# A gated delta-rule attention on one core: gate exponentials, the system's matrix and the attention weights at other places in the round

## The chip, the cores and the metric

The kernel runs on one core of a Trainium2 chip. Its time is the device time of one execution in microseconds; the median of several executions is compared. In a profile PE is TensorE (matmuls; PEld its weight loads), DVE is VectorE, ACT is ScalarE, POOL is GpSimd, and SP is SyncE, which here only issues DMAs. Each engine works through its own instructions in the order in which the program has them, and waits at semaphores that the others raise.

## The reference

Inputs are `x` (4 x 512 x 512), a side tensor of the same shape, a conditioning vector for each batch, and the weights. Two blocks are added to `x`: a mixing recurrence followed by a gated delta-rule attention (16 query/key heads, 32 value heads, head size 128), and the mixing recurrence again followed by a binarised linear layer. The kernel spends most of its time in the attention:

```python
q, k, v = conv4_silu(x @ Wq), conv4_silu(x @ Wk), conv4_silu(x @ Wv)    # causal, 4 taps
beta, g = sigmoid(b), -exp(A_log) * softplus(a + dt_bias)
q, k = rmsnorm(q), rmsnorm(k)                                           # scaled
decay = where(lower triangle, exp(g_i - g_j), 0)                        # g summed in the chunk
M = where(strictly lower, (beta * k) @ k.T * decay, 0)                  # the system's matrix
T = inverse(eye + M)
# over the chunks, with a state of 128 x 128:
v_new = T @ (beta * v) - (T @ (beta * k * exp(g))) @ state
out   = (q * exp(g)) @ state + (q @ k.T * decay) @ v_new                # attention weights
state = state * exp(g_last) + (k * exp(g_last - g)).T @ v_new
y = x + (rmsnorm(out) * norm_w * silu(z)) @ W_out
```

The reference takes chunks of 64 positions. The kernel computes the same sums with chunks of 128.

## The kernel before

The attention is a loop over 64 items, an item being one of 16 head groups (one query/key head with two value heads) of one of 4 batches. Each item has three stages, and a round of the loop does one stage each of three items: stage L of item `l` (query and key: projection, convolution, gates, the system's matrix), stage A of item `m` = `l` - 1 (value and gate projections, the inverse of the system), stage B of item `n` = `l` - 2 (the recurrence over 4 chunks, norm, output projection). There are 66 rounds; in all but the first and the last two all stages are there. `b` is the round's number modulo 4. It selects extra work for the second mixing block: `mix_exps` in rounds with b = 0, `mix_scale` (two copies) with b = 1, `mix_forward` and `mix_sums` with b = 2, `mix_inverse` (a logarithm, a copy and an exponential, with two loads of tables) and `mix_ratio` with b = 3. POOL splits the weights of `z` for a new head group at the start of a round with b = 1.

The order is written by hand. Every engine has a `body(l, m, n, b)`, on ACT and DVE with slots `k` = 0 to 19. The order of the rest of a round on PE is: the hops of the recurrence (`hop_u`, `hop_os`, `hop_kq`) between quarters of the projections of v and qk, then those of z, then, from slot 9 on, the 11 products of the inversion with output projections (`out`) and other small pieces between them. Product `j` stands in slot `9 + j`, and each needs the one before it, after its result has been brought from PSUM to SBUF. Products 4, 6, 7, 9 and 10 (`ADDED`) are finished by DVE (`finish_product`, lines 1180 to 1193), the others are copied by ACT (line 999), each for the two heads apart. Product 5 makes the fourth power (`lower` times `s2`, copied into `slot` `s0`), and product 6 waits for its copy, though it does not read it; products 6 and 7 are the last two corrections of the inverse (`pinv`), product 8 turns it, product 9 is the residual, and product 10 ends the inverse, which `hop_u` of the next round reads.

What builds the system and the gates for item `l`, in the second half of its round:

- `exp_decay` and `exp_small` on ACT (lines 938 to 970) turn the masked gates `gb` into `decay` in place, after a table load, and make two small vectors.
- `b_matrix` on DVE (lines 1161 to 1173) makes `kks` from the key products and then, for each head, the four blocks of `bt`, and raises `b_ready`.
- `attention_weights` on DVE (line 1177) multiplies the query-key products in PSUM bank `rc` by `decay`, and raises `attn_ready`.
- `off_blocks` on POOL (line 1297) makes `lower` from `bt`. SP's `gather_blocks` (lines 612 and 615) sends the 16 x 16 diagonal blocks to HBM and back as `block_in`. POOL's `invert_blocks` (lines 1321 to 1328) inverts them, and in the next round SP's `scatter_blocks` (lines 620 and 627) sends the inverses to HBM and back into `inv16`. Product 0 of the next round waits for them.
- SP's `load_gates` for the next item waits for `attn_ready`. POOL's `mask_gates` and, at b = 1, `split("z", ...)` stand behind `invert_blocks`.

The waits on which the order rests:

```python
pe.wait_ge(S["inv16_loaded"], (m + 1) * (16 * NB))     # product 0
W({"v": "wv_split", "z": "wz_split"}[kind], it // BATCH + 1)   # first quarter of v or z
await_product(pe, m, h, k - 1)                         # products 1 to 10
```

Of the kernel before, what the change touches and what calls it, by code (L numbers as in the profile page):

```python
# [475 lines left out]
def attention_phase(nc, ctx, t):  # L476

    with ExitStack() as c:
# [182 lines left out]
        def _(pe):  # L661
# [154 lines left out]
            def body(l, m, n, b):  # L816


                L, A, B, p = l is not None, m is not None, n is not None, b % 2

                def hop(f, ch):
                    if B:
                        f(n, p, ch)

                def proj(kind, i, *ks):
                    if (L if kind == "qk" else A):
                        for k in ks:
                            proj_quarter(kind, i, k, m, n, l, p if kind == "qk" else 1 - p)
# [3 lines left out]
                        out_half(n, m, l, j, h)  # L832

                proj("v", 0, 0, 1)
                if A:
                    W("attn_ready", 2 * m + 2)
                hop(hop_u, 0)
                proj("v", 0, 2, 3)
                hop(hop_os, 0)
                proj("v", 1, 0)  # L840
                hop(hop_kq, 1)
# [57 lines left out]
        def _(act):  # L899
# [88 lines left out]
            def body(l, m, n, b):  # L988
# [4 lines left out]
                for k in range(SLOTS):  # L993
# [19 lines left out]
                    if L:  # L1013
                        if k == 4:
                            tap0("qk", l, 0)
                        elif k == 6:
                            tap0("qk", l, 1)
                        elif k == 7:
                            if B:
                                W("kq_full", 3 * n + 3)  # L1020
                            silu("qk", l, 0, qkT2[p][:, 1, :])
                        elif k == 8:
                            silu("qk", l, 1, qkT2[p][:, 0, :])
                        elif k == 10:
                            query_squares(l)
                        elif k == 12:
                            exp_decay(l)
                        elif k == 13:
                            exp_small(l, p)
                    if A:  # L1030
                        if k == 8:
# [22 lines left out]
        def _(dve):  # L1054
            v = nc.vector
# [162 lines left out]
            def body(l, m, n, b):  # L1218
                L, A, B, p = l is not None, m is not None, n is not None, b % 2
                if A:  # L1220
                    dve.drain()
                    v_columns(m)
                if L:
                    qk_columns(l)
                for k in range(SLOTS):
# [27 lines left out]
                    if L:  # L1253
                        if k == 5:
                            conv_tap("qk", l, 0, 1)
                            conv_tap("qk", l, 0, 2)
                        elif k == 6:
                            conv_tap("qk", l, 0, 3)
                        elif k == 7:
                            conv_tap("qk", l, 1, 1)  # L1260
                            conv_tap("qk", l, 1, 2)
                        elif k == 8:
                            conv_tap("qk", l, 1, 3)
                        elif k == 10:
                            if b == 1:
                                mix_backward(*mix_unit(l))
                            elif b == 2:
                                mix_forward(*mix_unit(l))
                            key_sums(l)
                        elif k == 12:  # L1270
                            query_sums(l)
                            small(l, p)
                        elif k == 13:
                            b_matrix(l, 0, p)
                        elif k == 14:
                            b_matrix(l, 1, p)
                        elif k == 16:
                            attention_weights(l, 0, p)
                        elif k == 17:
                            attention_weights(l, 1, p)  # L1280
                    if B and k in (15, 16, 17):
                        add_out(n, {15: 0, 16: 1, 17: 2}[k])

# [306 lines left out]
```

## Time and profile before

| | us |
|---|---|
| median of three runs | 3532.75 |
| lowest and highest of them | 3524.03, 3534.42 |
| the profiled execution | 3526.48 |
| its span in the profile | 3524.8 |
| one round in the middle (product 0 to product 0) | 49.61 |

The profile's page gives busy time for each engine; over the span PE is busy for 3235.5 us (92%), DVE for 2574.7 us, ACT for 1981.9 us and POOL for 1597.5 us. A timeline lists instructions in order of time, with runs of like instructions merged: start, length from the first start to the last end, engine, line, what is written and read, count, and in brackets the idle time of the engine before it with what ended it. Instructions of one engine overlap a little in these records, so a row can start before the row above it has ended. The view of stretches gives busy time of each engine between two points in time and the granted clock of TensorE as a share of its full speed.

### The profile page before, as it was taken

Reading aid. Unit: us, or ns where it says so; the run is one execution under the profiler, and the core shown is the slowest. Engines: PE = TensorE matmul, PEld = TensorE weight load, DVE = VectorE, ACT = ScalarE, POOL = GpSimd, SP = SyncE. Lnnn points to the kernel's source line nnn. Section 1 sums busy time; section 2 is a strip of 40 time slices with the busy share of each in tenths; the row PEclk is TensorE's granted clock in tenths of the full one; section 3 lists DMA queues with packets and bytes.
Section 4 is the critical chain, followed back from the end, with each engine's and each line's share of the span. In section 5 each row is a group of like instructions: output and inputs, shape, how many; then the busy total and the mean of one; then the engine's idle time right before and its main releaser. Section 6 shows DMA issues by size and latency. Waiting matters only on the chain. (4 is left out here: it accounts for less than half of the span.)

```text
span 3524.8 us, 57286 instructions
## 1 busy us (share of the span) xinstructions
PE 3235.5 (92%) x18210; PEld 2523.2 (72%) x18210; DVE 2574.7 (73%) x5351; ACT 1981.9 (56%) x4826; POOL 1597.5 (45%) x2825
## 2 busy tenths in 40 slices
PE   0249999999999999999999999999999999999977
PEld 0237777777777777777777777777777777777753
DVE  7747777777777777777777777777777777777753
ACT  6735666555655665555555665555555665556531
POOL 7644535444454535444454535444454435444310
PEclk9989999999999999999999999999999999999998
DMA  3312222222222222222222222222222222322102
GB/s 120 119 53 76 84 75 68 76 80 76 72 64 81 85 75 63 82 79 73 73 66 81 85 74 60 85 78 72 69 72 81 85 74 57 83 83 69 51 8 107
DMA packets 295389, 265.68 MB, mean 75 GB/s; under 512 B 221584, under 2 KB 250384, under 8 KB 285840
## 3 DMA queue, kind: packets, MB, share of 16 engines
q1 hardware_dynamic: 286160, 131.99, 15.2%
q10 hardware_dynamic: 8928, 130.03, 10.0%
q8 instruction: 146, 2.39, 0.3%
q14 instruction: 155, 1.27, 0.1%
HBM read 232.30 MB, written 29.62 MB: 74 GB/s over the span
## 5 line engine op out<-in xcount | busy, mean ns | idle before, releaser
L689 PE MATMUL x<-xs,w_high 128*128 128x512 f32 x3072 | 1054.7, 424 | 24.0 <-POOL w_low L1338 13.6
L922 ACT ACTIVATE uvec<-rb,cpos 128x128 f32<-128x128 f32 x512 | 160.4, 364 | 861.9 <-PE rb L709 861.9
L689 PE MATMUL x<-xs,w_low 128*128 128x512 f32 x1536 | 608.5, 396 | 0.0
L689 PEld LDWEIGHTS x<-xs,w_high 128*128 128x128 f32 x3072 | 525.7, 191 | 88.0 <-POOL w_low L1338 14.0
L999 ACT ACTIVATE slot<-lane 128x512 fp32r<-128x512 f32 x640 | 363.5, 650 | 228.5 <-PE lane L813 228.5
L1321 POOL TENSOR_TENSOR block_step<-block_in 64x14 f32<-64x14 f32 (+6 forms) x896 | 231.2, 258 | 329.8 <-DMA block_in<-blocks_dram 208.5
L1378 POOL TENSOR_TENSOR rstd<-rarg,powers 128x8 f32<-128x8 f32 x64 | 106.1, 1657 | 529.5 <-DVE rarg L1115 529.5
L689 PEld LDWEIGHTS x<-xs,w_low 128*128 128x128 f32 x1536 | 289.8, 189 | 66.7
L813 PEld LDWEIGHTS lane<-pinv,slot 128*128 128x128 f32 x1536 | 199.7, 192 | 190.8 <-ACT slot L999 98.7
L1297 POOL TENSOR_TENSOR lower<-bt,offdiag 128x512 fp32r<-128x512 f32 x128 | 171.5, 1339 | 321.5 <-DVE bt L1171 321.5
L1078 DVE SCALAR_TENSOR_TENSOR cacc<-x,cwv,cacc 128x511 f32<-128x511 f32 (+2 forms) x384 | 281.7, 747 | 38.4 <-ACT cacc L909 3.7
L1078 DVE SCALAR_TENSOR_TENSOR cacc<-x,cwqk,cacc 128x511 f32<-128x511 f32 (+2 forms) x384 | 281.2, 745 | 27.1 <-ACT cacc L909 5.9
L1323 POOL TENSOR_TENSOR block_in<-block_in,block_step 64x14 f32<-64x14 f32 (+6 forms) x896 | 238.8, 267 | 131.1 <-issue 5.9
L813 PE MATMUL lane<-pinv,slot 128*128 128x128 f32 x1536 | 245.7, 299 | 51.8 <-ACT slot L999 47.0
L778 PE MATMUL x<-vT,w_out 128*128 128x512 f32 x512 | 278.4, 627 | 0.9 <-DVE vT L1159 0.9
L1104 DVE SCALAR_TENSOR_TENSOR wvec<-ra,egn,vtok 128x128 f32<-128x128 f32 x384 | 117.0, 346 | 171.0 <-PE ra L698 171.0
L1390 POOL TENSOR_TENSOR irk<-skt,powers 128x4 f32<-128x4 f32 x64 | 64.6, 1009 | 355.8 <-PE x L689 339.4
L1171 DVE SCALAR_TENSOR_TENSOR bt<-cacc,cneg,gb 128x128 f32<-128x128 f32 x512 | 210.8, 473 | 5.6 <-ACT gb L945 0.9
L931 ACT ACTIVATE junk<-oraw 128x128 f32<-128x128 f32 x512 | 159.0, 311 | 39.4 <-issue 1.0
L1153 DVE TENSOR_TENSOR oraw<-oraw,rstd 128x1024 f32<-128x1024 f32 x64 | 129.0, 2016 | 61.3 <-POOL rstd L1378 61.3
L1311 POOL TENSOR_TENSOR gb<-gb,causal 128x512 f32<-128x512 f32 x128 | 164.7, 1287 | 18.5
L1185 DVE TENSOR_TENSOR pinv<-lane,inv 128x512 fp32r<-128x512 f32 x128 | 82.5, 686 | 117.3 <-PE lane L813 117.3
(230 smaller groups left out, 7474.6 us busy)
## 6 DMA issues: line engine op xcount, KB each, us to landing
xs<-mix_dram ACTq DMA_DIRECT2D x62, 2048.0 KB, 7.8
gb<-cum_dram SPq DMA_DIRECT2D x128, 256.0 KB, 4.4
w_in<-in_w_qkvz SPq DMA_DIRECT2D x48, 512.0 KB, 4.1
w_out<-in_w_out SPq DMA_DIRECT2D x16, 512.0 KB, 5.0
blocks_dram<-bt SPq DMA_DIRECT2D x512, 8.0 KB, 1.5
inverse_dram<-block_out SPq DMA_DIRECT2D x64, 128.0 KB, 2.2
inv<-inverse_dram SPq DMA_DIRECT2D x512, 16.0 KB, 1.8
xacc<-in_x SPq DMA_DIRECT2D x4, 1024.0 KB, 11.5
```

Source lines behind the costliest of these rows:

```text
L689: ins = mm(PROJ_BANK[kind][i][:, :], w, x, start=(k == 0 and j == 0), stop=(k == KC - 1 and j == 2))
L778: ins = mm(OUT_BANK[j][:, :], w_out[:, h, sl(j, P)], hT[:, h, :], start=(h == 0), stop=(h == HPG - 1))
L813: ins = mm(lane[h][:, sl(ch, CH)], a, b, start=True, stop=True)
L922: ins = a(uvec[:, h, :], rb[:, sl(h, HD)], ACT.Copy, scale=sm2[p]["cpos"][:, ch, h:h + 1])
L931: ins = a(junk[:, :], oraw[:, ch, h, :], ACT.Square, accum_out=sm["oss"][:, ch, h:h + 1])
L999: a(DEST[job][:, h, :, :].rearrange("p c s -> p (c s)"), lane[h][:, :], ACT.Copy).then_inc(copied[h], 1)
L1078: ins = v.scalar_tensor_tensor(out=cacc[:, i, j:SEQ], in0=PROJ_BANK[kind][i][:, 0:SEQ - j], scalar=weights[:, i, 3 - j:4 - j], in1=cacc[:, ...
L1171: ins = v.scalar_tensor_tensor(out=pair[p][:, h, ch, :], in0=kks[:, ch, :], scalar=sm["cneg"][:, ch, h:h + 1], in1=decay[:, h, ch, :], op0 ...
L1297: ins = g.tensor_tensor(lower[:, h, :, :], pair[p][:, h, :, :], t["offdiag"][:, :].unsqueeze(1).to_broadcast([P, NCH, CH]), ALU.mult)
L1311: g.tensor_tensor(x, x, t["causal"][:, :].unsqueeze(1).to_broadcast([P, NCH, CH]), ALU.add).then_inc(S["masked"], 1)
L1321: g.tensor_tensor(step, block_in[:, 0:i, i:i + 1].to_broadcast(shape), block_in[:, i:i + 1, i + 1:BLK].to_broadcast(shape), ALU.mult)
L1323: g.tensor_tensor(block_in[:, 0:i, i + 1:BLK], block_in[:, 0:i, i + 1:BLK], step, ALU.add)
```

## The change

Three pieces of work are written at another place, and one wait is moved.

- On ACT `exp_decay` and `exp_small` (slots 12 and 13) both stand in slot 14, behind the copy of product 5.
- On DVE `b_matrix` (slots 13 and 14) stands in slot 16 for both heads, behind the finish of product 7.
- On DVE `attention_weights` (slots 16 and 17) opens the next round, ahead of `v_columns`.
- PE's wait for `attn_ready` stands behind `hop_u` and the rest of the first v projection instead of ahead of it.

No instruction of an engine is added or removed, apart from the order.

```diff
@@ tensor, body
                 proj("v", 0, 0, 1)
+                hop(hop_u, 0)
+                proj("v", 0, 2, 3)
                 if A:
                     W("attn_ready", 2 * m + 2)
-                hop(hop_u, 0)
-                proj("v", 0, 2, 3)
                 hop(hop_os, 0)
@@ scalar, body
-                        elif k == 12:
+                        elif k == 14:
                             exp_decay(l)
-                        elif k == 13:
                             exp_small(l, p)
@@ vector, body
                 if A:
+                    attention_weights(m, 0, 1 - p)
+                    attention_weights(m, 1, 1 - p)
                     dve.drain()
                     v_columns(m)
@@ vector, body
-                        elif k == 13:
+                        elif k == 16:
                             b_matrix(l, 0, p)
-                        elif k == 14:
                             b_matrix(l, 1, p)
-                        elif k == 16:
-                            attention_weights(l, 0, p)
-                        elif k == 17:
-                            attention_weights(l, 1, p)
```

How it moves instructions on DVE, from the finish of product 4 (L1185) to the first vectors of the next round, in a round of the middle. Before (L1166 and L1171 are `b_matrix`, L1187 the finishes of products 6 and 7, L1216 `add_out`, L1177 the attention weights, L1189 and L1191 the finishes of products 9 and 10):

```order
L1185 TENSOR_TENSOR pinv<-lane,inv 128x512 x2
L1166 TENSOR_TENSOR cacc<-x,strict 128x512
L1171 SCALAR_TENSOR_TENSOR bt<-cacc,cneg,gb 128x128 x8
L1187 TENSOR_TENSOR pinv<-lane,pinv 128x512 x2
L1216 TENSOR_TENSOR xacc<-xacc,x 128x512
L1187 TENSOR_TENSOR pinv<-lane,pinv 128x512 x2
L1177 TENSOR_TENSOR attn<-rc,gb 128x512
L1216 TENSOR_TENSOR xacc<-xacc,x 128x512
L1177 TENSOR_TENSOR attn<-rc,gb 128x512
L1216 TENSOR_TENSOR xacc<-xacc,ra 128x512
L1189 TENSOR_TENSOR slot<-lane,slot 128x512 x2
```

The same place in the changed kernel, whose line numbers on DVE are lower by one:

```order
L1184 TENSOR_TENSOR pinv<-lane,inv 128x512 x2
L1186 TENSOR_TENSOR pinv<-lane,pinv 128x512 x2
L1215 TENSOR_TENSOR xacc<-xacc,x 128x512
L1186 TENSOR_TENSOR pinv<-lane,pinv 128x512 x2
L1165 TENSOR_TENSOR cacc<-x,strict 128x512
L1170 SCALAR_TENSOR_TENSOR bt<-cacc,cneg,gb 128x128 x8
L1215 TENSOR_TENSOR xacc<-xacc,x 128x512
L1215 TENSOR_TENSOR xacc<-xacc,ra 128x512
L1188 TENSOR_TENSOR slot<-lane,slot 128x512 x2
L1215 TENSOR_TENSOR xacc<-xacc,rb 128x512
L1190 SCALAR_TENSOR_TENSOR bt<-pinv,lane 128x512 x2
L1176 TENSOR_TENSOR attn<-rc,gb 128x512 x2
```

The nine instructions of `b_matrix` now stand between the finish of product 7 and that of product 9, and the two of the attention weights behind the finish of product 10.

On ACT, in a round with b = 3, from the copy of product 3 (L999 `lower`) to `mix_inverse` (L959 to L962). Before:

```order
L999 ACTIVATE lower<-lane 128x512 x2
L945 ACT_TABLE_LOAD
L945 ACTIVATE gb<-gb,gneg 128x128 x8
L969 ACTIVATE edec<-edd 128x8
L970 ACTIVATE egl<-glast 128x8
L999 ACTIVATE slot<-lane 128x512 x2
L959 ACT_TABLE_LOAD
```

The same place in the changed kernel:

```order
L999 ACTIVATE lower<-lane 128x512 x2
L999 ACTIVATE slot<-lane 128x512 x2
L945 ACT_TABLE_LOAD
L945 ACTIVATE gb<-gb,gneg 128x128 x8
L969 ACTIVATE edec<-edd 128x8
L970 ACTIVATE egl<-glast 128x8
L959 ACT_TABLE_LOAD
```

The copy of product 5 passes the table load and ten exponentials, which then stand directly ahead of the mixing block's work and the copy of product 8.

## Rows read from the trace of the kernel before

**Rows 1.** Waits: who waited, for whom, total us, times, longest.
```profile
PE lane L813 <- ACT slot L999: 47.0, 63, 2.2
```
**Rows 2.** Stretches, a round each: length, busy us (instructions) by engine, clock, DMA.
```profile
1499.16:1548.77 49.61, 48.79 (x283) 38.30 (x282) 37.70 (x82) 27.06 (x71) 20.55 (x43) 1.00 0.23 62
```
**Rows 3.** Timeline, PE, products 5 to 7, 9 and 10: start, length us.
```profile
1510.71 1.07 PE L778 MATMUL x<-vT,w_out 128*128 128x512 f32 x2
1511.21 1.41 PE L813 MATMUL lane<-slot,lower 128*128 128x128 f32 x8
1512.46 1.07 PE L778 MATMUL x<-vT,w_out 128*128 128x512 f32 x2
1514.25 1.14 PE L813 MATMUL lane<-pinv,slot 128*128 128x128 f32 x8 [0.72 <-ACT slot L999]
1515.23 1.07 PE L778 MATMUL x<-vT,w_out 128*128 128x512 f32 x2
1516.37 1.26 PE L813 MATMUL lane<-pinv,slot 128*128 128x128 f32 x8
...
1520.98 1.95 PE L813 MATMUL lane<-slot,bt 128*128 128x128 f32 x16
...
1523.23 1.40 PE L813 MATMUL lane<-pinv,slot 128*128 128x128 f32 x8
```
**Rows 4.** Timeline, ACT, the same round: table load, then the copy of product 5.
```profile
1509.78 1.28 ACT L945 ACT_TABLE_LOAD   x1
...
1513.63 1.06 ACT L999 ACTIVATE slot<-lane 128x512 fp32r<-128x512 f32 x2
```
**Rows 5.** Timeline, DVE, the same round.
```profile
1511.66 0.68 DVE L1166 TENSOR_TENSOR cacc<-x,strict 128x512 f32<-128x512 f32 x1
...
1515.64 1.27 DVE L1187 TENSOR_TENSOR pinv<-lane,pinv 128x512 fp32r<-128x512 f32 x2
1516.84 0.67 DVE L1216 TENSOR_TENSOR xacc<-xacc,x 128x512 f32<-128x512 f32 x1
1517.43 1.27 DVE L1187 TENSOR_TENSOR pinv<-lane,pinv 128x512 fp32r<-128x512 f32 x2
...
1522.08 0.69 DVE L1189 TENSOR_TENSOR slot<-lane,slot 128x512 fp32r<-128x512 f32 x1 [0.98 <-PE lane L813]
```
**Rows 6.** One line, the blocks of `bt`: duration of one, ns, min/median/max.
```profile
L1171 DVE SCALAR_TENSOR_TENSOR bt<-cacc,cneg,gb x512: 336/347/1372, 222.1 to 3352.4; 128x128 f32<-128x128 f32 x171
```
**Rows 7.** Timeline, ACT, next round (b = 3): `mix_inverse`, the copy of product 8.
```profile
1564.31 1.28 ACT L959 ACT_TABLE_LOAD   x1
...
1569.44 1.09 ACT L999 ACTIVATE slot<-lane 128x512 fp32r<-128x512 f32 x2 [0.61 <-PE lane L813]
```
**Rows 8.** Timeline, SP: gather and scatter in the b = 2 round.
```profile
1515.74 3.62 SPq L612 DMA_DIRECT2D blocks_dram<-bt  x8
...
1537.64 3.76 SPq L627 DMA_DIRECT2D inv<-inverse_dram  x8
```
**Rows 9.** Timeline, SP: the scatter that follows a b = 1 round.
```profile
1687.35 4.84 SPq L627 DMA_DIRECT2D inv<-inverse_dram  x8
```
**Rows 10.** DMA issues: count, KB, median us to landing.
```profile
inv<-inverse_dram SPq DMA_DIRECT2D x512, 16.0 KB, 1.8
```
**Rows 11.** Timelines, POOL and PE, start of a b = 1 round: z's split, z's projection.
```profile
1636.33 2.38 POOL L1338 TENSOR_TENSOR w_low<-w_in,w_high 128x1024 fp32r<-128x1024 f32 x1
```
```profile
1643.94 0.71 PE L689 MATMUL x<-xs,w_high 128*128 128x512 f32 x2
```
**Rows 12.** Stretches at half and full clock, columns as in rows 2.
```profile
202.94:206.36 3.42, 3.42 (x9) 2.64 (x9) 0.20 (x3) 0.00 (x0) 0.00 (x0) 0.50 0.44 113
267.80:271.20 3.40, 2.41 (x16) 2.05 (x16) 2.00 (x4) 3.37 (x8) 0.25 (x1) 1.00 0.99 323
271.20:281.40 10.20, 8.31 (x36) 7.98 (x37) 7.52 (x15) 4.60 (x12) 2.84 (x3) 0.50 0.34 120
3442.00:3445.60 3.60, 0.88 (x3) 0.05 (x1) 0.69 (x1) 0.00 (x0) 0.00 (x0) 1.00 0.18 15
```

## The prediction

> **What bounds the kernel now.** I read the waits first, then one round cut out of the middle, then the timeline of that round engine by engine. The waits name one place where TensorE's matmuls stop in 63 rounds for 47.0 us together: product 6 stands behind ACT's copy of product 5 [rows 1]. A round takes 49.61 us, TensorE is busy for 48.79 us of it and its granted clock is 1.00 [rows 2]. So TensorE sets the round, and a chain that stays in its shade costs nothing. Read the timeline of PE as pairs: an output projection (L778, two matmuls) and the product behind it. Unhindered, the product ends 1.91 us after its pair began (1510.71 to 1511.21 + 1.41 = 1512.62). Product 6 ends 2.93 us after its pair (1512.46 to 1515.39), product 7 2.40 us (1515.23 to 1517.63) [rows 3]. So 1.02 + 0.49 = 1.5 us of each round are lost there, more than the 0.72 us that the brackets show. The first loss is ACT's: it loads a table at 1509.78, works through the exponentials and turns to the copy at 1513.63, 3.85 us later [rows 4], though product 5 had ended at 1512.62. The second is DVE's: it starts the finish of product 6 at 1515.64, when `b_matrix` has ended [rows 5].
>
> All points in time below are those of this round, which begins with product 0 at 1499.16 and is a b = 2 round.
>
> **The copy of product 5 goes first (gain).** The first head of product 5 ends half a product before its end, so ACT copies from about 1512.2 to 1513.3 (1.06 us [rows 4]). Product 6 then finds its first head copied by 1512.8 and starts unhindered: it ends at 1512.46 + 1.91 = 1514.37. DVE, with `b_matrix` gone from its front, starts the finish of product 6 at about 1513.95, and product 7 ends at about 1516.13. The 1.5 us are won by then. What is late next decides how much is kept.
>
> **`b_matrix` behind the finish of product 7 (gives most of it back).** DVE from there: finish 6 at 1513.95, `add_out` 1.20 later at 1515.15, finish 7 0.59 later at 1515.74, `b_matrix` 1.20 later at 1516.94 [rows 5]. The exponentials end at 1513.3 + 3.85 = 1517.15, which the first block of `bt`, 0.75 us after the start, does not feel. `b_matrix` occupies DVE from 1511.66 to 1515.64, 3.98 us; so it is over at 1520.92 and `b_ready` comes at about 1521.0, against 1515.74, where the gather starts [rows 5, 8]: **5.26 us later**. Two `add_out` of 0.6 us follow, so the finish of product 9 starts at 1522.12 and ends 0.69 us later at 1522.81. TensorE, 1.5 us early, would have wanted to start product 10 at about 1521.75; it starts at 1522.87, waits again a little for the second head (finished 0.6 us after the first, at 1523.42), and ends 0.65 us after that, at 1524.1 instead of 1523.23 + 1.40 = 1524.63. A usual round therefore keeps **0.53 us** of the 1.5. The finish of product 10 then ends about 1525.2, just before `hop_u` would start.
>
> **Attention weights in the next round (nothing).** They cost DVE 2 x 0.6 us behind the finish of product 10 and end at about 1526.4. Only `hop_os` reads them, which on TensorE follows `hop_u`, its copy and half a projection, a microsecond later. DVE has 2.6 us idle there before its first hop. SP's load of the next gates waits for them, but the gates are not touched before POOL's inversion is over. I take zero, with an upper bound of 0.1 us a round.
>
> **ACT at b = 3 (loss).** There `mix_inverse` stands behind the exponentials. It starts at 1564.31 and ends 0.61 us before the copy of product 8 at 1569.44, so it takes 4.52 us [rows 7]; moved to the clock of the first round by 49.61 us, that copy starts at 1519.83. In the changed kernel ACT ends the exponentials at 1517.15 and `mix_inverse` at 1521.7, and the copy is 1.86 us later than before, where TensorE would have been 1.5 us earlier. Its first head ends at 1522.3, and product 9 starts at 1522.35 instead of 1520.98 [rows 3]. The rest runs as before: the round is **1.36 us longer**, with TensorE idle for some 2.6 us in it (from the output projection behind product 8, which ends at about 1519.7). At b = 0 and b = 1 the mixing work is short (`mix_exps`, two copies) and ends near 1518.5, in time.
>
> **The inverses' round trip.** It is rigid: gather, inversion, scatter, product 0. The last DMA of the scatter is issued about 0.45 us before 1537.64 + 3.76 = 1541.40 and lands 1.8 us later [rows 8, 10], at 1542.8, and product 0 of the next round starts at 1548.77 [rows 2]: 6.0 us of room. The move takes 5.26 and an earlier TensorE 0.53, so 0.2 us is left. From uneven landings I expect 0.08 us lost in a usual round, leaving 0.45. Behind b = 1 rounds the eight loads took 4.84 us instead of 3.76 [rows 9] and the gather was slower too: there the room is only 4.1 us. If that stays, that round has 5.26 + 0.53 - 4.1 = 1.7 us to wait. Both long groups fall on moments at which code is fetched, and those go with TensorE, not with `b_ready`, so I expect the slowness not to stay in this round.
>
> **z's weights at b = 1.** POOL's split stands behind the inversion and ended at 1638.71; z's first matmul started at 1643.94 [rows 11], 5.23 us later. Room 5.23 against 5.26 + 0.53: a stall of about 0.6 us, up to 1.2 if DMAs are slow there. This round interval changes by +0.1 to +0.6; I take +0.35.
>
> **The sum.** Of four rounds: two usual ones, -0.45 each; b = 3, +1.36; the one with z's split, +0.35. Over the attention: 16 x (-0.90 + 1.36) + 15 x 0.35 = **+12.6 us**.
>
> **TensorE's clock.** The idle 2.6 us at b = 3 are of a kind the trace shows at one place. In 267.80 to 271.20, with products alone and gaps, TensorE was busy for 2.41 us of 3.40, and the clock then fell to 0.50 of full, 1.2 GHz, for 10.2 us. After 0.88 us busy of 3.60 it fell too. The shortest stretch at the low level lasted 3.4 us [rows 12]. The full rounds, with a gap of 0.72 us, kept 1.00 [rows 2]. The new gap lies with the first group. A fall costs half of what it lasts, 1.7 to 5.1 us. TensorE has gapless work behind the gap, so I take 2.5 us, and that it happens in half of the 16 rounds: 8 x 2.5 = **+20 us**.
>
> The Trainium skill ("TensorE: Matmul & The Clock Gate", section "Why this matters for your kernels") warns of idle gaps between bursts of matmuls that are somewhat longer than the one I foresee. By that rule the clock would stay and the sum be +12.6; no row here has a gap of just this length.
>
> Together +32.6 us on the profiled execution's 3526.48 (its span is 3524.8; 1.7 us lie around it), that is 3559. That execution was at the low end of the runs; on the median of 3532.75 it gives **3565 us**.
>
> **Rivals.**
>
> 1. *The clock stays up.* All else as above: 3532.75 + 12.6 = 3545. For it: no fall anywhere between the second and the last round, and the skill's rule. Against it: rows 12. Chance 0.25.
>
> 2. *The round trip binds.* If the slow DMAs stay behind b = 1 rounds, each costs 1.7 us more, 16 x 1.7 = 27 us; if `b_ready` comes 0.5 us later than worked out, all four kinds of round feel it, 0.5 x 63 = 31 us. With half the clock's loss: 3573 to 3592. For it: only 0.2 us of room. Chance 0.15.
>
> 3. *Faster: `b_matrix` is short in its new place.* One block of `bt` takes 347 ns at the median and one of eight takes up to 1372 [rows 6], just while POOL begins `lower`. Were that pause absent, `b_matrix` would take 2.9 us. Then the finish of product 9 would be in time and usual rounds keep 1.5 us; with b = 3 unchanged the sum is 16 x (-1.5 x 2 - 1.1 + 1.36) = -44 us: 3489 before any fall of the clock, some 3505 with it. It decides from about 0.5 us less than 3.98. Against it: POOL starts `lower` on the first head's `b_ready` wherever that is, so the pause should move along. Chance 0.12.
>
> 4. *No change.* Stalls and gains cancel: the b = 3 copy is late by less than a microsecond. Chance 0.08, near 3533.
>
> **How the numbers follow.** My forecast has 0.40. The forecast and rival 2 are slower, 0.55, and so are four fifths of rival 1 (its 12.6 us have 6 to 20 around them, from z's stall and the loss in usual rounds), 0.20: 0.75 for slower by over 0.3%, which is 10.6 us and about what a measurement of this kernel can tell from no change. Same: 0.13. Faster: 0.12. The range leaves out rival 3 and the far end of rival 2: 3533 to 3590.
>
> **What would show it.** In the profile after: no wait of product 6 for ACT; product 10 waiting for the finish of product 9 for about 1.1 us in usual rounds; a row of 2.6 us idle before product 9 once in four rounds, ended by ACT's copy; z's first matmul waiting for POOL's `w_low` at b = 1; rounds of 49.1, 49.1, 51.0 and 49.9 us; granted clock below 1.00 in some of the b = 3 rounds. I would be wrong if the copy of product 8 is in time at b = 3, or if product 0 waits for DMAs in most rounds.

## The result and the profile after

| | before | after |
|---|---|---|
| median of four runs, us | 3532.24 | 3557.51 |
| lowest and highest, us | 3524.03, 3534.42 | 3553.84, 3561.81 |
| profiled execution, us | 3526.48 | 3553.84 |
| its span, us | 3524.8 | 3551.8 |

The change makes the kernel slower by 25 us; the ratio of the times is 1.0076 [1.0058, 1.0094]. The forecast was 3565 us with a range of 3533 to 3590.

The page of the changed kernel. TensorE is busy for 9.5 us less than before, and the span is 27.0 us longer:

```profile
PE 3226.0 (91%) x18210; PEld 2542.7 (72%) x18210; DVE 2567.7 (72%) x5351; ACT 1988.1 (56%) x4826; POOL 1585.7 (45%) x2825
```

Two rounds of it as stretches, product 0 to product 0, first one with b = 2, then one with b = 3 (columns as in rows 2):

```profile
2106.40:2155.05 48.65, 48.14 (x280) 38.30 (x281) 37.24 (x81) 26.51 (x70) 19.32 (x43) 1.00 0.24 73
2155.05:2207.59 52.54, 49.83 (x283) 39.48 (x282) 36.94 (x80) 31.49 (x76) 26.16 (x45) 0.97 0.29 78
```

This usual round is 1.0 us shorter than the 49.61 us of rows 2, the one with b = 3 is 2.9 us longer, and its granted clock is 0.97. The next table has all 62 rounds between the first product 0 that has a full round behind it and the last, taken from the starts of product 0 in the two traces. Falls are the stretches in which the granted clock is 0.50; "held" counts the rounds whose next product 0 starts less than 0.16 us after the last load of the inverses has landed:

| b | rounds | before, mean us | after, mean us | after, median us | falls after | held, before | held, after |
|---|---|---|---|---|---|---|---|
| 1 | 15 | 49.62 | 49.38 | 49.44 | 0 | 0 | 12 |
| 2 | 16 | 49.70 | 48.97 | 48.90 | 1 | 0 | 8 |
| 3 | 16 | 49.62 | 51.93 | 52.32 | 11 | 0 | 0 |
| 0 | 15 | 49.62 | 50.04 | 49.95 | 0 | 0 | 1 |

Together 15 x (-0.24) + 16 x (-0.73) + 16 x 2.31 + 15 x 0.42 = +28.0 us, against +27.0 in the spans.

The waits of the changed kernel (who waited, for whom, total us, times, longest). The 63 waits of rows 1 for the copy of product 5 are gone; what stands in their place is 17 waits for ACT, 46 for DVE's finish of product 9, 16 for POOL's split and 15 for the DMAs of the inverses:

```profile
PE lane L813 <- ACT slot L999: 43.5, 17, 2.7
...
PE x L689 <- POOL w_low L1334: 26.3, 16, 13.6
PE lane L813 <- DVE slot L1188: 22.6, 46, 0.8
...
PE lane L813 <- DMA inv<-inverse_dram: 8.7, 15, 1.4
```

The timeline of PE in the round from 2106.40, from product 6 to product 10 (it answers to rows 3). Products 6 and 7 each follow their pair by 0.51 us and end 1.92 us after it began; product 10 waits 0.48 us for DVE:

```profile
2119.45 1.07 PE L778 MATMUL x<-vT,w_out 128*128 128x512 f32 x2
2119.96 1.41 PE L813 MATMUL lane<-pinv,slot 128*128 128x128 f32 x8
2121.20 1.07 PE L778 MATMUL x<-vT,w_out 128*128 128x512 f32 x2
2121.71 1.41 PE L813 MATMUL lane<-pinv,slot 128*128 128x128 f32 x8
...
2126.47 1.95 PE L813 MATMUL lane<-slot,bt 128*128 128x128 f32 x16
2128.26 1.02 PE L778 MATMUL rb<-vT,w_out 128*128 128x512 f32 x2
2129.77 1.26 PE L813 MATMUL lane<-pinv,slot 128*128 128x128 f32 x8 [0.48 <-DVE slot L1188]
```

The timeline of DVE there (it answers to rows 5): finish 7, `kks`, the eight blocks of `bt`, two `add_out`, finish 9 without a pause between them:

```profile
2122.76 1.28 DVE L1186 TENSOR_TENSOR pinv<-lane,pinv 128x512 fp32r<-128x512 f32 x2
2123.96 0.68 DVE L1165 TENSOR_TENSOR cacc<-x,strict 128x512 f32<-128x512 f32 x1
2124.71 3.21 DVE L1170 SCALAR_TENSOR_TENSOR bt<-cacc,cneg,gb 128x128 f32<-128x128 f32 x8
2127.84 0.67 DVE L1215 TENSOR_TENSOR xacc<-xacc,x 128x512 f32<-128x512 f32 x1
2128.44 0.67 DVE L1215 TENSOR_TENSOR xacc<-xacc,ra 128x512 f32<-128x512 f32 x1
2129.04 1.27 DVE L1188 TENSOR_TENSOR slot<-lane,slot 128x512 fp32r<-128x512 f32 x2
```

The next round has b = 3. ACT's timeline, where three table loads stand in a row of work without a gap, ahead of the copy of product 8 (it answers to rows 4 and 7):

```profile
2168.08 1.08 ACT L999 ACTIVATE slot<-lane 128x512 fp32r<-128x512 f32 x2 [2.45 <-PE lane L813]
2169.18 1.28 ACT L945 ACT_TABLE_LOAD   x1
2170.48 2.45 ACT L945 ACTIVATE gb<-gb,gneg 128x128 f32<-128x128 f32 x8
...
2173.14 1.28 ACT L959 ACT_TABLE_LOAD   x1
...
2175.73 1.28 ACT L962 ACT_TABLE_LOAD   x1
...
2177.56 1.06 ACT L999 ACTIVATE slot<-lane 128x512 fp32r<-128x512 f32 x2
```

What TensorE does meanwhile, and the stretches at that place (columns as in rows 2). It idles for 2.68 us ahead of product 9, then 3.4 us go by at half the clock:

```profile
2174.44 1.07 PE L778 MATMUL rb<-vT,w_out 128*128 128x512 f32 x2
2178.19 3.01 PE L813 MATMUL lane<-slot,bt 128*128 128x128 f32 x16 [2.68 <-ACT slot L999]
```
```profile
2175.70:2179.10 3.40, 0.91 (x8) 0.91 (x9) 2.28 (x5) 2.88 (x4) 2.65 (x3) 1.00 0.08 8
2179.10:2182.50 3.40, 3.40 (x14) 2.57 (x12) 1.38 (x2) 0.00 (x0) 0.26 (x1) 0.50 0.11 11
```

### The profile page after: what moved, and what is told of

Same layout as the page of the kernel before. It is cut to its first block and busy times, and to the rows that moved or that the text cites. A ratio compares the mean times of both kernels' runs of the same rounds, so it can differ in the third digit from the quotient of the medians.

```text
span 3551.8 us, 57224 instructions
## 1 busy us (share of the span) xinstructions
PE 3226.0 (91%) x18210; PEld 2542.7 (72%) x18210; DVE 2567.7 (72%) x5351; ACT 1988.1 (56%) x4826; POOL 1585.7 (45%) x2825
## 5 line engine op out<-in xcount | busy, mean ns | idle before, releaser
L689 PE MATMUL x<-xs,w_high 128*128 128x512 f32 x3072 | 1054.8, 424 | 37.1 <-POOL w_low L1334 26.3
L999 ACT ACTIVATE slot<-lane 128x512 fp32r<-128x512 f32 x640 | 359.5, 636 | 194.0 <-PE lane L813 191.7
L813 PE MATMUL lane<-pinv,slot 128*128 128x128 f32 x1536 | 265.9, 313 | 22.8 <-DVE slot L1188 22.6
L1186 DVE TENSOR_TENSOR pinv<-lane,pinv 128x512 fp32r<-128x512 f32 x256 | 164.5, 683 | 141.9 <-PE lane L813 141.9
L813 PEld LDWEIGHTS lane<-slot,bt 128*128 128x128 f32 x1024 | 136.8, 210 | 79.4 <-ACT slot L999 68.2
L813 PE MATMUL lane<-slot,bt 128*128 128x128 f32 x1024 | 141.3, 297 | 43.5 <-ACT slot L999 43.5
```

The source lines that it names most:

```text
L689: ins = mm(PROJ_BANK[kind][i][:, :], w, x, start=(k == 0 and j == 0), stop=(k == KC - 1 and j == 2))
L813: ins = mm(lane[h][:, sl(ch, CH)], a, b, start=True, stop=True)
L999: a(DEST[job][:, h, :, :].rearrange("p c s -> p (c s)"), lane[h][:, :], ACT.Copy).then_inc(copied[h], 1)
L1186: ins = v.tensor_tensor(pinv[:, h, :, :], made, pinv[:, h, :, :], ALU.add)
```

## The experiments

Theory: four things make the time, which the runs below switch one by one. TensorE wins back the wait for the copy of product 5; ACT's mixing work at b = 3 opens a gap, and the gap makes the clock fall; POOL's split of z is late at b = 1; the round trip of the inverses has no room left. The rivals are that the gap alone costs and the clock nothing, and that `b_matrix` behind product 7 is the cause by itself. Ratios are to the kernel before on the same chip. A change against the changed kernel is the difference of the two ratios.

**The exponentials alone, in the kernel before.** `b_matrix` stays in slots 13 and 14.

```diff
-                        elif k == 12:
+                        elif k == 14:
                             exp_decay(l)
-                        elif k == 13:
                             exp_small(l, p)
```

> The kernel before with only ACT's part of the change: the exponentials in slot 14, behind the copy of product 5; the system's matrix stays in slots 13 and 14 on DVE, the attention weights in 16 and 17. Theory (the copy's place can be had only with the matrix moved): product 6 starts unhindered, but DVE stands in b_matrix until the exponentials are there, about 3.3 us later than before, and the finish of product 6 with it; TensorE idles some 3 us before product 7 in each round and its clock falls in most of them. 3.2 us a round and up to 1.6 for the clock: +200 to +300 us on the kernel before. Rival (the exponentials are what made the kernel slow, the matrix is free): like the changed kernel, +27 us.

3876.19 us, ratio 1.0981 [1.0947, 1.1014], +343 us. DVE's timeline: the first block of `bt` waits for the exponentials, with the finishes of product 6 queued behind it. PE's timeline: product 7 waits for them.

```profile
2029.62 0.68 DVE L1165 TENSOR_TENSOR cacc<-x,strict 128x512 f32<-128x512 f32 x1
2033.87 3.31 DVE L1170 SCALAR_TENSOR_TENSOR bt<-cacc,cneg,gb 128x128 f32<-128x128 f32 x8 [3.57 <-ACT gb L945]
2037.11 1.27 DVE L1186 TENSOR_TENSOR pinv<-lane,pinv 128x512 fp32r<-128x512 f32 x2
```
```profile
2037.84 1.81 PE L813 MATMUL lane<-pinv,slot 128*128 128x128 f32 x8 [4.60 <-DVE pinv L1186]
```

A round takes 55.0 us, 5.4 more than before, and each of the 62 has a fall of the clock. That is more than expected: TensorE idles 4.6 us before product 7 (290.7 us in 63 waits) where some 3 were foreseen, and 39 of 63 falls last 6.8 us where the working had 1.6 us of loss, one of 3.4. The first two pieces of the change are one: the exponentials can't go behind the copy unless `b_matrix` goes behind product 7.

**The matrix and the attention weights alone.** The changed kernel with `exp_decay` and `exp_small` back in slots 12 and 13.

```diff
-                        elif k == 14:
+                        elif k == 12:
                             exp_decay(l)
+                        elif k == 13:
                             exp_small(l, p)
```

> The changed kernel with the exponentials back in slots 12 and 13 on ACT, ahead of the copy of product 5; the system's matrix and the attention weights stay where the change puts them. Theory (the gain is the copy's, the matrix alone only delays): product 6 waits for ACT again (0.7 us in the brackets, 1.0 in all), the mixing block's inverse at b = 3 is in time, so no round of 52 us and no fall of the clock; the matrix is ready about 6.3 us later than in the kernel before, so the inverses' round trip binds product 0 in most rounds: 0.3 to 0.5 us more in usual rounds, 1 to 2 where DMAs are slow. Sum +30 to +60 us on the kernel before. Rival (the loss of the change is the matrix's delay and not ACT's at b = 3): then this kernel is at least as slow as the changed one with rounds of 51 us or more at b = 3.

3570.21 us, ratio 1.0118 [1.0103, 1.0133], +43 us, within the 30 to 60 expected. Both waits of PE stand side by side, ACT's from before and DVE's from after:

```profile
PE lane L813 <- ACT slot L999: 47.0, 63, 2.2
...
PE lane L813 <- DVE slot L1189: 28.0, 63, 0.8
```

The usual round takes 49.84 us, 0.22 more than before, and 50.24 at b = 1 and 50.83 at b = 0. Product 0 is held by the landing in 31 of 62 rounds. Rounds with b = 3 take 49.87 us; only one has a fall of the clock, late in the last of them. So `b_matrix` in the new place is a loss by itself (the attention weights stand in the next round here too; their place is tested below), and the round of 52 us is not its doing. The copy's new place wins 0.97 us in a usual round (48.87 against 49.84) and pays for it at b = 3.

**`mix_inverse` behind the copy of product 8.**

```diff
-                        elif b == 3:
-                            mix_inverse(*mix_unit(l))
+                    if L and k == 17 and b == 3:
+                        mix_inverse(*mix_unit(l))
```

> The changed kernel with mix_inverse on ACT (b = 3) in slot 17, behind the copy of product 8, instead of slot 15. Theory (at b = 3 the copy of product 8 stands behind the exponentials and mix_inverse, and the idle gap of 2.7 us also makes the clock fall): the gap before product 9 goes, b = 3 rounds fall from a mean of 51.9 us to 48.7 to 49.0, no fall of the clock between the second and the last round; 16 x 3.0 = 48 us less than the changed kernel, so 20 to 25 us less than the kernel before. Rival (the loss at b = 3 is DVE's or the DMAs', and the clock falls by itself): nothing moves, within 5 us of the changed kernel.

3505.84 us, ratio 0.994 [0.9921, 0.9959], -21 us, as expected. Rounds with b = 3 take 48.88 us at the median instead of 52.32, and no fall of the clock is left in the place of the old gap. Two are left elsewhere: one of 3.4 us behind a wait of 3.1 us for z's weights, one of 6.8 us near the end of the loop. So the three pieces of the change are a gain once ACT's mixing work is out of the way: what made it a loss is the b = 3 round, 16 x (51.93 - 49.06) = 46 us in means.

**z's split ahead of `off_blocks`, a round earlier.**

```diff
-                if l is not None and b == 1:
-                    split("z", l // BATCH)
                 if l is not None:
+                    if b == 0:
+                        split("z", l // BATCH)
                     off_blocks(l, m, b % 2)
```

> The changed kernel with POOL's split of z's weights for a new head group in the b = 0 round, ahead of off_blocks, where POOL waits for the matrix, instead of behind the inversion at the start of the b = 1 round. Theory (z's first matmul waits 0.9 us for this split once in four rounds): the wait goes, and the interval from b = 0 to b = 1 shrinks from a mean of 50.04 us by 0.9 at most, since the inverses land 1.0 us before product 0 there: 15 x 0.9 = 13 us less than the changed kernel, 3544. Rival (the inverses' round trip sets this interval anyway): under 3 us less.

3547.90 us, ratio 1.0056 [1.0039, 1.0072]: some 7 us less than the changed kernel, where 13 were expected. The wait for `w_low` is gone, and the wait for the inverses has grown from 15 times to 18 and from 8.7 us to 25.6 (14.6 of it a single one ahead of the steady rounds):

```profile
PE lane L813 <- DMA inv<-inverse_dram: 25.6, 18, 14.6
```

The b = 0 rounds went from 50.04 to 49.37 in means, 0.67 us for a stall of 0.85: in 10 of the 15 the next product 0 is now held by the landing. That is 10 of the 13 us, and rounds with b = 2 gave 2 more. The b = 3 rounds took 5 back (52.24 against 51.93): two of their falls last 6.8 us, and one of 10.2 us comes near the end of the last of them.

**Both, and `kks` early.** `mix_inverse` and the split as in the last two, and the first instruction of `b_matrix`, which makes `kks`, alone back in slot 13 as `strict_keys`.

```diff
+                        elif k == 13:
+                            strict_keys(l)
                         elif k == 16:
                             b_matrix(l, 0, p)
```

> The changed kernel with mix_inverse behind the copy of product 8, z's split early (as in the two other runs), and the first step of b_matrix (the key products times the strict mask, kks), which needs no decay, back in slot 13, where DVE is idle. Theory: b_ready and the finish of product 9 come 0.75 us earlier, product 10 no longer waits; usual rounds fall from 48.65 to about 48.2 us where TensorE sets them, and by 0.75 us where the round trip does (b = 1: 49.6 to 48.9); b = 3 about 48.2. Mean 48.4, 63 x 1.2 = 76 us less than the kernel before: 3455, ratio 0.978. Rival (DVE's lateness is not what holds product 10): the sum of the other two runs, about 35 us less than the kernel before.

3448.88 us, ratio 0.9781 [0.9758, 0.9804], -78 us, as expected (-76). Product 10 no longer waits for DVE. Rounds take 48.14 us (b = 1: 49.20), and product 0 is held by the landing in 39 of 62. Four of these rounds have a fall, each behind a wait of 1.4 to 2.0 us for the inverses. The inverses are the limit now:

```profile
PE lane L813 <- DMA inv<-inverse_dram: 32.7, 22, 14.6
```

**The gap before product 9 shorter, and longer.** First the scaling of `mix_q` moved from `mix_inverse` to behind the copy of product 8; then instead one more copy added in `mix_inverse` (it takes one instruction of ACT's more; its result is not used).

```diff
-                a(mix_q[:, :], mix_q[:, :], ACT.Copy, scale=t["scale"][:, b:b + 1])
...
+                    if L and k == 17 and b == 3:
+                        mix_rescale(*mix_unit(l))
```
```diff
                 a(mix_q[:, :], mix_q[:, :], ACT.Copy, scale=t["scale"][:, b:b + 1])
+                a(mix_e[:, 1, :], mix_s[:, :], ACT.Copy)
                 act.drain()
```

> The changed kernel with one of mix_inverse's instructions, the copy that scales mix_q (0.6 us of ACT), behind the copy of product 8. The idle gap before product 9 at b = 3 becomes 2.1 us instead of 2.7. Theory (TensorE's clock falls because of this gap, in some of the rounds): b = 3 rounds without a fall shrink from 50.8 to 50.2 us, and the falls, 11 of 16 b = 3 rounds in the changed kernel, become clearly fewer (0 to 6). 10 us from the gap and 8 to 16 from the clock: 18 to 26 us less than the changed kernel. Rival (the falls come from something else, or from any gap): still about 11 falls, 10 us less.

> The changed kernel with one more copy of 128x512 on ACT inside mix_inverse (into a half of mix_e that is free at b = 3). The gap at b = 3 becomes 3.3 us. Theory (the gap makes the clock fall, more surely the longer it is): a fall in 15 or 16 of the 16 b = 3 rounds, rounds without one 51.4 us, with one 52.9; 16 x 0.6 + 5 x 1.6 = 18 us more than the changed kernel. Rival: 10 us more, falls as before.

3546.44 us, ratio 1.0045 [1.0029, 1.006], and 3573.53 us, 1.0129 [1.0113, 1.0144]. Against the changed kernel's 1.0076 that is about -11 and +19 us. The waits for ACT, of the shorter, then of the longer:

```profile
PE lane L813 <- ACT slot L1002: 33.8, 17, 2.1
```
```profile
PE lane L813 <- ACT slot L1000: 52.0, 17, 3.2
```

| gap at b = 3, longest, us | rounds with a fall | with, median us | without, median us |
|---|---|---|---|
| 2.1 | 6 of 16 | 51.86 | 50.21 |
| 2.7 | 11 of 16 | 52.52 | 50.92 |
| 3.2 | 14 of 16 | 53.05 | 51.33 |

Rounds with and without a fall differ by 1.6 to 1.7 us, at each of the three lengths. The rival that only the gap costs is out. The counts are of one profiled execution each. Three other kernels here have the same gap of 2.7 us, with falls in 10, 12 and 9 of 16 rounds, so 6 against 11 alone would show little; 6 and 14 at the two ends, against 42 of 64 between them, do show that the length counts. The shorter gap gave less than expected (18 to 26 us): its profiled execution, at the upper end of its runs, has two falls of 6.8 us at other places, ahead of z's projection and near the end.

**Attention weights back between the finishes.** In slots 16 and 17 as before, in the changed kernel.

```diff
-                    attention_weights(m, 0, 1 - p)
-                    attention_weights(m, 1, 1 - p)
...
                             b_matrix(l, 1, p)
+                            attention_weights(l, 0, p)
+                        elif k == 17:
+                            attention_weights(l, 1, p)
```

> The changed kernel with the attention weights back in slots 16 and 17 on DVE, behind the system's matrix and ahead of the finish of product 9. Theory (the finish of product 9 is DVE's next late instruction, and each 0.1 us put ahead of it is paid by TensorE, while the place at the start of the next round is free): the finish of product 9 comes 1.2 us later, product 10 waits 1.7 us instead of 0.5, rounds with b = 1 and b = 2 grow from 48.65 to 49.85 us where TensorE sets them; b = 3 hardly changes, since ACT is later there. +0.6 to +1.2 us in about 47 rounds: 30 to 55 us more than the changed kernel. Rival (the attention weights cost the same in either place): within 5 us of the changed kernel.

3648.71 us, ratio 1.0341 [1.032, 1.0363], some 93 us above the changed kernel where 30 to 55 were expected. Its waits, and one of them in the timeline of PE:

```profile
PE lane L813 <- DVE slot L1188: 77.7, 46, 2.0
PE lane L813 <- ACT slot L999: 43.8, 17, 2.7
```
```profile
2136.20 1.26 PE L813 MATMUL lane<-pinv,slot 128*128 128x128 f32 x8 [1.68 <-DVE slot L1188]
```

Product 10 waits 1.68 us instead of 0.48, in 46 rounds 77.7 us instead of 22.6, or +55. The rest is the clock: 45 of 62 rounds have a fall, 33 more, and at 1.6 us each that is +53. Against that the wait for z's weights is gone, -13 (12.9 us in one wait instead of 26.3 in 16). Where there is none a round takes 50.06 to 50.32 us, with one 51.64 to 51.67 (b = 3: 50.93 and 53.66). Of the 46 rounds whose one long gap is the 1.7 us before product 10, 36 have a fall; of the 16 with 2.7 us before product 9, 9 have one. So the length of a gap alone doesn't say how often the clock falls. Product 0 is held by the landing nowhere.

**POOL's `lower` waits for both heads.** First in the kernel with all three of the early pieces, then in the changed kernel alone. It tests rival 3, the block of `bt` that takes 1.37 us.

```diff
-                    pool.wait_ge(S["b_ready"], 2 * l + h + 1)
+                    pool.wait_ge(S["b_ready"], 2 * l + 2)
```

> The version with everything early (e5) in which POOL's first instruction of off_blocks waits for both heads of the matrix instead of the first. Theory (one block of bt is stretched by 1.0 us because POOL begins lower beside it, and the inverses' round trip, 0.14 us before product 0 in 39 of 62 rounds of e5, is what b_ready sets): the stretched block falls from 1.37 to 0.35 us, b_ready comes 1.0 us earlier, rounds bound by the round trip shrink by up to 1 us to TensorE's own 47.9 us: mean 48.0, 30 us less than e5, ratio 0.969 to the kernel before. Rival (the stretch is DVE's own, or POOL's part of the chain moves instead): no change against e5.

3437.34 us, ratio 0.9745 [0.973, 0.9759], -90 us: the fastest of all, and faster than both kernels. The eight blocks of `bt` take 2.18 us in its timeline instead of 3.21:

```profile
1770.16 2.18 DVE L1171 SCALAR_TENSOR_TENSOR bt<-cacc,cneg,gb 128x128 f32<-128x128 f32 x8
```

One block of the 512 is stretched (1983 ns), instead of one in every round. Rounds take 47.96 to 48.02 us at the median; product 0 is held in 12 of 62. The gain over the kernel without it is some 12 us and not the 30 expected. Behind the first round no product waited for DVE in either, so the microsecond counts only where the inverses' round trip binds: 39 rounds before, 12 after, for 0.15 to 0.2 us each at b = 0, 2 and 3, and the slow loads behind b = 1 still hold 8 of 15.

> The changed kernel with one wait changed: POOL's off_blocks waits for both heads of the matrix. This is my third rival brought about: the matrix without the stretched block, 2.2 us instead of 3.2. By the prediction's arithmetic: the finish of product 9 is in time, product 10 does not wait, usual rounds 48.65 to about 48.1; the round trip gains 1.0 us, so rounds that it sets shrink by as much; z's wait (0.9 us) goes; b = 3 keeps its 51.9 us with the falls of the clock. b = 1: 49.4 to 48.4, b = 2: 49.0 to 48.2, b = 0: 50.0 to 49.0: 15 x 3 = 45 us less than the changed kernel, 18 us less than the kernel before, ratio 0.995. Other view (the stretch only moves to a later instruction of DVE): no change against the changed kernel.

3522.11 us, ratio 0.997 [0.9957, 0.9983], -11 us, with 18 expected. The blocks of `bt` in the view of one line (ns, min/median/max; it answers to rows 6), none of which is stretched:

```profile
L1170 DVE SCALAR_TENSOR_TENSOR bt<-cacc,cneg,gb x512: 340/344/353, 221.6 to 3346.8; 128x128 f32<-128x128 f32 x171
```

The usual round takes 47.94 us, 0.96 less than in the changed kernel. The b = 3 round has not moved, 52.48 us, since there TensorE waits for ACT's copy and not for DVE: in the waits the row for ACT still reads 43.6 us, and what TensorE waits for z's weights has become longer.

```profile
PE lane L813 <- ACT slot L999: 43.6, 17, 2.7
PE x L689 <- POOL w_low L1334: 29.4, 16, 13.5
```

Its profiled execution is the slowest of ten, 3528.87 us, and the rounds say what is missing in it. Those with b = 3 have grown by 0.44 us in the mean (52.37), since four of the twelve falls last 6.8 us instead of 3.4. Those with b = 0 have won 0.50 us (49.54) and not 1.0: z's wait has grown, and two more falls come where z's projection waits (52.11 us against 48.91). That is some 7 us each. Stretches of one of the long ones: it sets in while TensorE still idles (product 9 starts at 2554.69), where the fall of the changed kernel shown above set in 0.9 us after the gap:

```profile
2553.60:2557.00 3.40, 2.31 (x11) 2.31 (x12) 0.20 (x1) 1.52 (x3) 2.47 (x3) 0.50 0.17 19
2557.00:2560.40 3.40, 3.40 (x12) 2.37 (x11) 1.37 (x3) 0.00 (x0) 0.64 (x3) 0.50 0.07 19
```

## Why the prediction was right, point by point

The side, the mechanism and the four kinds of round came out as forecast: 49.1, 49.1, 51.0 and 49.9 us were named, and the medians are 49.44 (b = 1), 48.90 (b = 2), 50.92 (b = 3, without a fall) and 49.95 (b = 0). The gain of the usual round was put too low and what the round trip costs too low as well, and these cancel in part. The loss to the clock came out right by two factors that were off in opposite ways.

**The copy of product 5: right.** 1.5 us were foreseen by the end of product 7. From product 0 it ends at 18.46 us before and at 16.93 after in b = 2 rounds that no wait opens, 1.53 less; in those that open behind a wait of TensorE's it ends at 16.72. There product 5 already ends 0.2 us earlier (13.22 against 13.42). Why is not shown; that other engines catch up during the wait would fit. The round shown above is one of these, so its product 6 ends at 14.97 us where the working has 15.21.

**`b_matrix` behind product 7: right in kind, too dear.** In the round shown above, from product 0, working against trace: gather at 21.84 against 21.55 (before 16.58), finish 9 at 22.96 against 22.64, product 10 at 23.71 against 23.37, its end at 24.94 against 24.63. The whole chain came 0.2 us earlier, then another 0.1. Kept at the end of product 10 were 0.84 us in this round and 0.64 in one that no wait opens (24.83), instead of 0.53; in the length of a round that nothing holds, 0.97 us (48.65) and 0.76 (48.86). The forecast wait of product 10 of about 1.1 us is there as well, though the bracket reads 0.48 us of idle: product 10 starts 1.51 us after its pair began, and before it was 0.46, with 1523.23 in rows 3 for the product and this row for the pair:
```profile
1522.77 1.02 PE L778 MATMUL rb<-vT,w_out 128*128 128x512 f32 x2
```

That the matrix is to blame for the rest was shown by moving one instruction of it back (with `kks` early, a usual round takes 48.14).

**Attention weights: nothing, as foreseen**, and no row of TensorE's waits for them. Their old place would have cost 93 us; the prediction did not price it, and the expectation of that run, 30 to 55, was too low.

**b = 3: right.** 1.36 us longer and 2.6 us idle were foreseen. Rounds without a fall of the clock are 1.30 us longer (50.92), and TensorE idles 2.68 us. With `mix_inverse` behind the copy both are gone.

**The round trip: the room was right, what followed from it only in part.** Foreseen were 0.2 us of room and 0.08 us of loss in a usual round. The step that fails is "so I expect the slowness not to stay in this round". The gather's slowness did go: its eight DMAs take 3.62 us at the median in b = 1 rounds, where they took 4.47. The loads' stayed in part: 4.41 us at the median and up to 5.18, against 4.85 before, and slow (above 4.4) in 8 of 15 rounds. In SP's timeline of one of them:

```profile
1896.29 0.46 SPq L620 DMA_DIRECT2D inverse_dram<-block_out  x1
1898.54 5.17 SPq L627 DMA_DIRECT2D inv<-inverse_dram  x8
```

They held the next product 0 in 12 of 15 rounds, so that kind won 0.24 us instead of 0.45. The waits there are 0.54 us in the mean and 1.44 at most. They didn't come to the 1.7 us of rival 2, since the gather was 0.85 us faster, the loads 0.4, and `b_ready` 4.97 us later, not 5.26. Where the split of z no longer stood in the way, the round trip bound at b = 0 too, as 10 of 15 rounds showed.

**z's split: a size off.** The stall was put at 0.6 to 1.2 us and was 0.91 in the row below (PE's timeline, start of a b = 1 round), 0.85 in the mean of the 15 behind the first. The round interval grew by 0.42 where +0.35 was taken.

```profile
2052.59 0.73 PE L689 MATMUL x<-xs,w_high 128*128 128x512 f32 x2 [0.91 <-POOL w_low L1334]
```

**The clock: right in kind, and in size by luck.** 8 falls of 2.5 us were foreseen. 12 came (11 at b = 3, one behind a wait for the inverses), each 3.4 us long and worth 1.6 (52.52 against 50.92): 19 us instead of 20. A fall cost half of what it lasts, as in the working; I had put its length between 3.4 and 10.2 us. That too few falls were each put too dear, so that the product fits, is luck. The Trainium skill ("TensorE: Matmul & The Clock Gate", section "Why this matters for your kernels") warns only of longer gaps. The measurement decides: the clock fell in 11 of 16 rounds at 2.7 us, in 6 at 2.1, and in 36 of the 46 rounds with a gap of 1.7 in the kernel with the attention weights back.

**The sum.** Without the falls the rounds give 28 - 19 = +9 us, against +12.6: the free rounds won more, the held ones gave some of it back. With the falls 27.4 us between the two profiled executions, against 32.6.

**Rivals.** 1, the clock stays up: refuted by the falls. 2, the round trip: it holds 21 of 62 rounds, but TensorE waits only 8.7 us for it in all. (The 3573 to 3592 us given for this rival are the sum with none and with all of the clock's loss, not with half.) 3, the short `b_matrix`: the stretched block moved along with POOL's `lower`, as argued against it (rows 6; its maximum after is 1367 ns). With that block gone the kernel is faster than before by 11 us, which is the rival's sign but not its size (28 us with the clock's loss). Against the kernel before, its rounds with b = 2 won 1.79 us and those with b = 1 1.14, where 1.5 was taken for both; those with b = 0 won 0.08 and not 1.1, since z's weights came too late, and those with b = 3 lost 2.75, the gap and the clock.

## What to carry to other kernels

A piece of work that is moved behind a critical step pushes everything that was behind it: check each kind of round for what then stands ahead of the next critical step, since the one round in four with extra work decided the sign here (-0.6% with that work moved too, +0.8% without). Where a chain is won back, look at which waits come next in line; with all three of them moved, the same idea was worth 2.2%, and 2.6% with POOL's read out of DVE's way. A gap on TensorE costs its own length, and where the clock falls 1.6 us on top. It fell behind 6 of 16 gaps of 2.1 us and behind 36 of 46 gaps of 1.7, so a step that is late by two microseconds has to be priced at about three.

## What the runs showed of the hardware

**The clock falls after shorter gaps than I had expected.** A gap of 2.1 us before product 9 was followed by a fall in 6 of 16 rounds, one of 2.7 in 42 of 64 (four kernels), one of 3.2 in 14 of 16. A gap of 1.7 us before product 10 was followed by one in 36 of 46 rounds, so the place counts beside the length; what it is about the place was not tested. Waits of 1.4 us for the inverses were followed by a fall too, in two kernels. The 12 falls between the rounds of the changed kernel lasted 3.4 us. In other kernels 16 of the falls around the gap at b = 3 lasted 6.8 us, and each of these began while TensorE was still idle, 0.6 to 1.1 us before the gap ended; most of the shorter ones began after it. Near the end of the loop falls of 6.8 and 10.2 us came in rounds behind several waits of 0.7 to 1.0 us with no longer one close by.

**An instruction of POOL's that reads SBUF holds one of DVE's.** One block of `bt` takes 344 ns, and 1367 when POOL's `lower` starts just ahead of it; that instruction of POOL's takes 1.3 us. In the changed kernel with POOL held back until both heads are done, no block took over 353 ns. The Trainium skill ("SBUF — State Buffer", section "Who interferes with whom") says that a DVE instruction with two inputs in SBUF contends with a GpSimd instruction that reads SBUF, and that the second one then waits for the first to end. The runs agree: the block is held for 1367 - 344 = 1023 ns, by an instruction that had begun a little earlier and takes 1.31 us. POOL's timeline in the round shown above:

```profile
2125.93 1.31 POOL L1293 TENSOR_TENSOR lower<-bt,offdiag 128x512 fp32r<-128x512 f32 x1 [9.60 <-DVE bt L1170]
```

**Slow issues of DMAs go with the fetching of code.** One of the eight loads takes 0.43 us to issue. Of 1024 issues of gathers and scatters, those above 0.8 us were 10 in the changed kernel and 34 in the kernel before; all 10, and 32 of the 34, overlap a transfer on the queue that fetches instructions (q8, of the kind `instruction`, in the page's list of DMA queues). Another 10 and 25 issues overlap one too and take 0.8 us or less. That the slow ones coincide with fetches is what the records show; that the one causes the other was not tested. The slow loads behind b = 1 are such ones: in the kernel before all 15 groups of eight have an issue above 0.8 us (4.43 to 5.14 us for eight), in the changed kernel 8 of 15 (4.41 to 5.18).
